# Two distance layers of a fused four-layer kernel: weights written at another place, squares and box sums in parts, three taps of the second half ahead of the products of sums

## The reference

```python
def _conv_dt(x, centers):                       # centers: [O, C*9]
    patches = lax.conv_general_dilated_patches(x, filter_shape=(3, 3), ..., padding=((1, 1), (1, 1)))
    p = patches.transpose(0, 2, 3, 1).reshape(-1, C * 9)
    p2 = jnp.sum(p * p, axis=-1, keepdims=True)
    c2 = jnp.sum(centers * centers, axis=-1)
    d2 = p2 - 2.0 * (p @ centers.T) + c2
    d = jnp.sqrt(jnp.maximum(d2, D2_EPS))
...
out = jax.nn.relu(_bn(_conv_dt(x, centers1), gamma1, beta1))
out = _bn(_conv_dt(out, centers2), gamma2, beta2)
return jax.nn.relu(out + x)
```

## Time and profile before

| | |
|---|---|
| median of 3 runs | 768.92 us (766.22 to 769.92) |
| profiled execution | 763.28 us |
| its span in the trace | 761.1 us |
| mean granted TensorE clock | 0.915 of full speed |
| last addition of the deformable layer ends | 670.07 us |
| first distance layer, first tap to last statistics | 672.36 to 704.03 us |
| second distance layer, first tap to last statistics | 714.63 to 749.09 us |

### The profile page before, as it was taken

The page is one execution under the profiler, slowest core; times in us unless marked ns, Lnnn a source line. Parts: engine busy times, 40 slices in busy tenths (PEclk is TensorE's granted clock), DMA queues, the critical chain, the costliest instruction groups (busy, mean ns, idle before and its releaser), DMA issues.

```text
span 761.1 us, 29083 instructions
## 1 busy us (share of the span) xinstructions
PE 591.4 (78%) x13260; PEld 412.2 (54%) x13260; DVE 627.5 (82%) x811; ACT 486.0 (64%) x680; POOL 144.3 (19%) x246
## 2 busy tenths in 40 slices
PE   2628999699886799888886779678888888467591
PEld 1215788484653576666554555456666655345260
DVE  5997999993457999999998336899999999795356
ACT  2715565223227999999993413899999999332514
POOL 1013000000241333334200034133344320000000
PEclk9959999899987899999999798899999999879596
DMA  5013000000678788887720068889788770000002
GB/s 202 0 29 84 4 3 4 18 4 19 170 225 346 244 287 273 267 275 259 247 93 3 3 183 265 315 242 340 239 262 266 270 258 14 2 2 3 1 3 111
DMA packets 30197, 111.10 MB, mean 146 GB/s; under 512 B 11140, under 2 KB 15940, under 8 KB 25976
## 3 DMA queue, kind: packets, MB, share of 16 engines
q0 software_dynamic: 14912, 87.85, 34.1%
q1 hardware_dynamic: 15160, 21.36, 9.3%
HBM read 92.19 MB, written 19.65 MB: 147 GB/s over the span
## 4 chain that ended last, share of the span: by engine, by line
DVE 29%; PE 26%; ACT 25%; issue 8%; DMA 8%; SPq 3%; POOL 0%; DVEq 0%; ACTq 0%; POOLq 0%
PE psum L1438 7%; ACT arena L1201 6%; DVE arena L709 5%; ACT arena L1211 5%; ACT arena L1200 5%; PE psum L1587 4%; DMA offsets<-arena 4%; PE psum L1385 4%; PE psum L1472 4%; DMA arena<-offsets_by_batch 3%; ACT arena L1184 3%; ACT arena L1191 3%; PE psum L1496 2%; SPq L508 2%; DVE arena L837 2%
## 5 line engine op out<-in xcount | busy, mean ns | idle before, releaser
L1472 PE MATMUL psum<-arena 64*64 64x297 f32 (+4 forms) x4512 | 231.8, 350 | 55.5 <-DVE arena L837 45.7
L1472 PEld LDWEIGHTS psum<-arena 64*64 64x64 f32 x4512 | 170.8, 138 | 124.7 <-DVE arena L837 63.3
L1664 POOL DMA_DIRECT2D arena<-offsets_by_batch x128 | 79.4, 633 | 210.9 <-DVE arena L837 150.2
L1438 PE MATMUL psum<-arena 32*32 32x512 f32 x2304 | 88.4, 657 | 20.4 <-issue 14.5
L1385 PE MATMUL psum<-arena 32*32 32x512 f32 x2592 | 96.3, 614 | 8.1 <-DVE arena L689 8.1
L835 DVE SCALAR_TENSOR_TENSOR arena<-arena 128x792 f32<-128x792 f32 (+3 forms) x96 | 92.6, 964 | 12.0 <-ACT arena L1201 11.0
L1211 ACT ACTIVATE arena<-psum 128x792 f32<-128x792 f32 (+1 forms) x96 | 89.4, 931 | 14.5 <-PE psum L1477 9.0
L1201 ACT ACTIVATE arena<-arena 128x792 f32<-128x792 f32 (+3 forms) x96 | 93.4, 973 | 0.0
L1200 ACT ACTIVATE arena<-arena 128x792 f32<-128x792 f32 (+3 forms) x96 | 93.1, 970 | 0.0
L837 DVE SCALAR_TENSOR_TENSOR arena<-arena 128x792 f32<-128x792 f32 (+3 forms) x96 | 92.4, 962 | 0.0
L836 DVE SCALAR_TENSOR_TENSOR arena<-arena 128x792 f32<-128x792 f32 (+3 forms) x96 | 92.3, 962 | 0.0
(11 more groups left out here) (161 smaller groups left out, 726.0 us busy)
## 6 DMA issues: line engine op xcount, KB each, us to landing
arena<-offsets_by_batch POOLq DMA_DIRECT2D x112, 576.0 KB, 8.0
arena<-offsets_by_batch POOLq DMA_DIRECT2D x16, 624.0 KB, 7.6
offsets<-arena SPq DMA_DIRECT2D x32, 256.0 KB, 10.5
offsets_by_batch<-offsets SPq DMA_DIRECT2D x184, 24.0 KB
arena<-columns POOLq DMA_DIRECT2D x24, 160.0 KB, 9.6
columns<-arena POOLq DMA_DIRECT2D x8, 320.0 KB
arena<-in_x SPq DMA_DIRECT2D x4, 512.0 KB, 5.3
out<-arena SPq DMA_DIRECT2D x8, 256.0 KB, 2.2
```

Source lines behind the costliest of these rows:

```text
L1438: ins = t_.matmul(ps_q(2 * axis + h, conv_bank(m) + i), cols(W_CONV[L] + (axis * K + t) * Q, Q, Q * i, Q), ap(XA + (BLK * m + 8 * h + t // ...
L1472: ins = t_.matmul(ps_t(s, bank + r, first * K * w, many * K * w), window, ap(g_at(unit, d0) + first * TW + s * w, [[GS + TW, many], [SLOTS ...
```

## The change

- `distance_weights(0)` moves from behind the deformable layers to the start of the second of them, ahead of `bound_offsets`. Its weights lie where the first deformable layer's weights were. `distance_weights(1)` moves between the two halves of the first distance layer.
- First distance layer: squares in two parts (35 and 33 rows) and box sums in two parts (34 and 32 rows).
- Input of the second layer: pairs 0 and 1 on ScalarE as before, pairs 2 and 3 on VectorE (`second_input`: a multiply-add and a maximum).
- Second distance layer: the squares of each pair's 16 inner rows by themselves, pairs 0 and 1 ahead of ScalarE's border copies and pairs 2 and 3 behind them, then those of the border rows; box sums in the same five parts.
- TensorE takes the taps in the order 3 to 8, then 0 to 2. In the second layer it waits for the border copies only ahead of the seventh tap. Three taps of the second half stand ahead of the first half's products of sums.

```diff
+        W_DT = [place(K * P, MATS), place(K * P, SAMP)]
+        JUNK = [MATS + K * P, SAMP + K * P]
+        SPLIT = PW // 2 + 1
...
             def layer2(L):
+                if L == 1:
+                    distance_weights(0)
                 bound_offsets(L, 0)
...
+            def box(L, rows, pitch, src, dst):
+                sq = lambda dx: ap(src + dx, [[pitch, rows], [1, W]])
+                hs = ap(dst, [[W, rows], [1, W]])
+                link(v.tensor_tensor(hs, sq(0), sq(1), ALU.add))
+                return v.tensor_tensor(hs, hs, sq(2), ALU.add)
+            def boxes_of_images():
+                for part, (first, end) in enumerate(((0, SPLIT), (SPLIT, PW))):
+                    dve.wait_ge(s_sq, part + 1)
+                    box(0, end - first, XW, SQ3 + (first + 1) * XW + 1, HS3 + first * W).then_inc(s_box, 1)
+            def boxes_of_pairs():
+                for i in range(4):
+                    dve.wait_ge(s_sq, 2 + i + 1)
+                    box(1, REGION, PW, SQ3 + i * PAIRN + PW, HS3 + (i * RP + 1) * W).then_inc(s_box, 1)
+                dve.wait_ge(s_sq, 7)
+                sq = lambda dx: ap(SQ3 + dx, [[PAIRN, 4], [(RP - 1) * PW, 2], [1, W]])
+                hs = ap(HS3, [[RP * W, 4], [(RP - 1) * W, 2], [1, W]])
                 link(v.tensor_tensor(hs, sq(0), sq(1), ALU.add))
                 v.tensor_tensor(hs, hs, sq(2), ALU.add).then_inc(s_box, 1)
...
+                    if L == 0 and c == 0:
+                        distance_weights(1)
...
+            def second_input():
+                dve.wait_ge(s_cz, 1)
+                dve.wait_ge(s_coef, 4)
+                part = lambda i: ap(XP3 + i * PAIRN + PW + 1, [[PW, REGION], [1, W]])
+                for i in (2, 3):
+                    ins = v.tensor_scalar(part(i), ap(D3 + 2 * i * CH, [[W, REGION], [1, W]]), cols(NC_, 1),
+                                          cols(NC_ + 1, 1), ALU.mult, ALU.add)
+                link(ins)
+                for i in (2, 3):
+                    v.tensor_scalar(part(i), part(i), 0.0, None, ALU.max).then_inc(s_x3v, 1)
...
-            dve.wait_ge(s_xa, 3 * NCH)
-            distance_weights(0)
-            distance_weights(1)
+            boxes_of_images()
             distance(0)
+            second_input()
             copy_lower_borders()
+            boxes_of_pairs()
             distance(1)
...
-                    act.wait_ge(s_xa, 3 * NCH)
-                    a.activation(cols(SQ3, XN), cols(XA, XN), ACT.Square).then_inc(s_sq, 1)
+                    for first, end in ((0, SPLIT + 1), (SPLIT + 1, XW)):
+                        act.wait_ge(s_xa, 2 * NCH + (5 if first == 0 else NCH))
+                        a.activation(cols(SQ3 + first * XW, (end - first) * XW), cols(XA + first * XW, (end - first) * XW),
+                                     ACT.Square).then_inc(s_sq, 1)
                 else:
+                    inner = lambda buf, i: cols(buf + i * PAIRN + PW, REGION * PW)
+                    act.wait_ge(s_x3, 2)
+                    for i in range(2):
+                        a.activation(inner(SQ3, i), inner(XP3, i), ACT.Square).then_inc(s_sq, 1)
                     act.wait_ge(s_hp, 2)
...
                     ins.then_inc(s_ha, 1)
+                    act.wait_ge(s_x3v, 2)
+                    for i in (2, 3):
+                        a.activation(inner(SQ3, i), inner(XP3, i), ACT.Square).then_inc(s_sq, 1)
                     act.wait_ge(s_ha, 1)
                     act.wait_ge(s_hv, 1)
-                    a.activation(cols(SQ3, 4 * PAIRN), cols(XP3, 4 * PAIRN), ACT.Square).then_inc(s_sq, 1)
+                    border = lambda buf: ap(buf, [[PAIRN, 4], [(RP - 1) * PW, 2], [1, PW]])
+                    a.activation(border(SQ3), border(XP3), ACT.Square).then_inc(s_sq, 1)
...
-                    for i in range(4):
+                    for i in range(2):
...
-                pe.wait_ge(s_x3, 4)
+                pe.wait_ge(s_x3, 2)
+                pe.wait_ge(s_x3v, 2)
...
-                for c in range(2):
-                    for k in range(K):
+                def taps(c, first, end):
+                    for step in range(first, end):
+                        k = (step + 3) % K
+                        if L == 1 and step == 6 and c == 0:
+                            pe.wait_ge(s_ha, 1)
+                            pe.wait_ge(s_hv, 1)
...
-                        pe.wait_ge(s_box, L + 1)
+                        pe.wait_ge(s_box, 2 if L == 0 else 7)
...
+                taps(0, 0, K)
+                if L == 1:
+                    pe.wait_ge(s_d2, NCH)
+                taps(1, 0, 3)
+                norms(0)
+                taps(1, 3, K)
+                norms(1)
...
                     move_borders()
-                    pe.wait_ge(s_ha, 1)
-                    pe.wait_ge(s_hv, 1)
```

More of the change, by code:

```diff
@@ L306, in build @@
         s_hp, s_ha, s_hv = sem("border_rows_moved"), sem("borders_by_scalar"), sem("borders_by_vector")
-        s_x3, s_fin, s_res = sem("second_input_ready"), sem("final_sums_ready"), sem("results_ready")
+        s_x3, s_x3v = sem("second_input_by_scalar"), sem("second_input_by_vector")
+        s_fin, s_res = sem("final_sums_ready"), sem("results_ready")
         block = ctx.enter_context(nc.Block())
@@ L389, in build @@
         assert OUT3 + N <= XA
-        W_DT = [place(K * P, SAMP), place(K * P, SAMP + K * P)]
-        JUNK = SAMP + 2 * K * P
+        W_DT = [place(K * P, MATS), place(K * P, SAMP)]
+        JUNK = [MATS + K * P, SAMP + K * P]
+        assert (K + 2) * P <= (2 + NT) * P + NGRP * Q
+        SPLIT = PW // 2 + 1
         def xa_rows(ch):
@@ L998, in distance_weights @@
                                 ALU.mult).then_inc(s_dw3, 1)
-                link(v.tensor_tensor_reduce(cols(JUNK, K * C), cols(WR + WREP[f"cn{L}"][0], K * C),
+                link(v.tensor_tensor_reduce(cols(JUNK[L], K * C), cols(WR + WREP[f"cn{L}"][0], K * C),
                                             cols(WR + WREP[f"cn{L}"][0], K * C), 1.0, 0.0, ALU.mult, ALU.add,
@@ L1040, in _, with distance @@
                 layer2(L)
[L1043 to L1051, removed]
+            def box(L, rows, pitch, src, dst):
[14 more added lines that the diff above has]
+                hs = ap(HS3, [[RP * W, 4], [(RP - 1) * W, 2], [1, W]])
                 link(v.tensor_tensor(hs, sq(0), sq(1), ALU.add))
                 v.tensor_tensor(hs, hs, sq(2), ALU.add).then_inc(s_box, 1)
+            def distance(L):
                 for c in range(2):
@@ L1587, in distances, with norms @@
                                 t_.matmul(ps_q(j, 4 * c + i), cols(W_DT[L] + k * P + Q * i, Q, Q * i, Q), at,
-                                          start=(k == 0), stop=False)
+                                          start=(step == 0), stop=False)
+                def norms(c):
                     if c == 0:
-                        pe.wait_ge(s_box, L + 1)
+                        pe.wait_ge(s_box, 2 if L == 0 else 7)
                     for ky in range(3):
```

## The result

| | before | after |
|---|---|---|
| median of the runs | 767.57 us (4 runs) | 753.79 us (749.62 to 754.98, 4 runs) |
| ratio of the runs | | 0.9845, 95% interval 0.9807 to 0.9883 |
| profiled execution, its span | 763.28, 761.1 us | 754.98, 753.1 us |
| mean granted clock | 0.915 | 0.924 |

The direction is right, and every step is there, but the sum is too small, and the 768.92 us that it was taken from lay high.

The account below looks back on a forecast made before the run. No single engine was taken to bound the kernel; its last 92 us were a chain of waits hardly overlapping. Gains of 2.2 + 3.1 + 1.7 = 7.0 us, from a 768.92 us median, gave 761.9 us, range 758 to 766.5.

Parts of the forecast that it names:

- Part 1 and 2: First distance layer: weights written earlier start the taps 2.2 us sooner; split squares and box sums keep that gain.
- Nothing waits: First distance layer of the kernel before: nine taps end as the box sums end, about 683.6 us, without any wait.
- 0.38 us: Both distance layers: cost of each further microsecond of TensorE at 1.2 GHz, from taps of 1.70 against 1.06 us.
- Part 3: Second distance layer's input split between ScalarE and VectorE: ready after 3.0 us instead of 4.65, 1.6 us earlier.
- T+3.1: Second distance layer: start of the border products, 3.1 us after T, the moment the coefficients are there.
- Rival B: VectorE's new instructions run at the full-length rate: second input 5.0 instead of 3.0 us, total 763.9 us; chance 0.08.
- Part 4: Second layer's taps start before the border copies: 3.1 us earlier, 1.6 from the split input and 1.5 from the copies.
- Border products: T+3.1 to T+4.3: Second layer: border products take 1.19 us after the input is ready, and TensorE's taps begin at T+4.3.
- Part 5: Second layer's squares and box sums in five parts: TensorE's 1.7 us standstill before the products of sums is gone.
- rival A: TensorE's clock rises when it did though taps start earlier: 2.0 us less gain, 763.9 us; chance 0.20.
- Rivals C and D: C: a misjudged wait undoes parts 3 to 5, 766.7 us, 0.09; D: 1.2 GHz through both first halves, 773.5 us, 0.03.

Follow-up runs that it names:

- e9: Changed kernel with the first distance layer's weights written behind the last addition of the deformable layers again; 755.78 us, ratio 0.9859 to the kernel before.
- e3: Kernel before with only the placement of both distance layers' weights changed; 765.83 us, ratio 1.0012 to the kernel before.
- e1: Kernel before run again without any edit, beside itself; 765.87 us against 764.18, ratio 1.0014.
- e16: Kernel before, unedited, one profiled execution for a fifth trace; 93.6 us behind the last addition of the deformable layers.
- e10: Kernel before with four filler products ahead of TensorE's wait for the second layer's box sums; ratio 0.9994 to the kernel before.
- e13: Kernel before with filler products on TensorE between the distance layers, around the group sum and behind the border products; 764.62 us, ratio 0.9991.
- e7: Changed kernel with the second layer's squares in one instruction and its box sums whole again; 756.26 us, ratio 0.9875 to the kernel before.
- e6: Changed kernel with the second layer's wait for border copies ahead of the first tap, not the seventh; 757.39 us, ratio 0.9888 to the kernel before.
- e12: Changed kernel run a third time without any edit; 753.36 us, ratio 0.9856 to the kernel before.
- e5: Changed kernel with the second layer's input written by ScalarE alone in four pieces; 756.61 us, ratio 0.9890 to the kernel before.
- e4: Changed kernel with no taps of the second half ahead of the first half's products of sums; 758.17 us, ratio 0.9889 to the kernel before.
- e2: Changed kernel run again without any edit; 752.06 us, ratio 0.9831 to the kernel before.
- e15: Kernel before, unedited, one profiled execution for a fourth trace; 93.0 us behind the last addition of the deformable layers.
- e8: Changed kernel with filler products keeping TensorE busy ahead of both distance layers; 751.52 us, ratio 0.9804 to the kernel before.
- e11: Kernel before run a third time without any edit; 764.95 us, ratio 0.9989 to the kernel before.

## Why the prediction was wrong

The mechanisms were right; two terms of the sum were too small. One charged taps with a wait that only the border copies have. The other was read from a single trace and took the profile's idle time for the whole loss.

**Part 1 and 2, 2.2 us: right in the mean.** Stage A shows 2.3 (means), e9 1.9, and e3 shows that without the parts none of it arrives. Two readings behind it were off. "Nothing waits" in the kernel before hid a wait: its first products of sums began at 683.66, 0.05 us behind the box sums, while the last product of the nine taps, 0.59 us long, ended at 683.92 and so had begun 0.3 us before these. Its stage A stays at 28.9 us for low stretches of 3.0 to 4.2 us (before, e1, e16, e10, e13) and is longer only at 5.4 and 5.8 (29.2, 29.3). And a microsecond of the low clock costs more than 0.38 us where TensorE waits for nothing: stage A of the changed kernel's versions goes from 25.9 at 3.0 us (e7) to 27.5 at 6.2 (e6), 0.5 us for each. So the gain of the stage depends on the clock: in after's trace, with 5.8 us low, it is 1.6 us against before's, in e12's, with 3.4, it is 2.8.

**Part 3, 1.6 us: right.** The multiply-adds took 0.77 us and the maxima 0.65, for 0.75 and 0.69 forecast; T+3.1 for the border products is what the trace shows (709.28 - 706.17). e5 gives 1.7. Rival B is out.

**Part 4, "3.1 us earlier": mis-sized, 4.3.** The step that failed is "Border products: T+3.1 to T+4.3", with the taps behind it. The 1.19 us from the earlier trace rows run from the first border product to the copies, which read what these products write. The taps read none of it for six steps: they entered 0.05 us behind the first border product. e6 sizes the edit at 2.6 us where 1.5 was charged; with the 1.7 of e5 that is the 4.3 of stage B.

**Part 5, "the standstill of 1.7 us": mis-sized, about 4.** This is the larger of the two failed steps. The standstill was taken from one trace, which had the longest low stretch of the five (6.0 us), so the slowest taps and the shortest standstill. The five show 1.71, 1.80, 2.65, 2.67 and 3.09 us, 2.4 on average. In three of them the clock fell behind it, and the first operation of VectorE came 4.8, 4.8 and 5.8 us behind the first product of sums in place of 3.2: 1.2 us on average over the five. That makes 3.5 of the 4.1 us of stage C. The other 0.6 is what the idle time leaves out: the profile counts it from the end of the taps' last product, 727.07 in before's trace, and this product, 0.59 us long, began at 726.48, so from start to start it is 2.3 us and not 1.71. Without a wait this tail costs nothing: in after's trace the first products of sums (723.78) come ahead of a tap's product that starts at 723.92. It is the oversight of part 4 once more, with the same figure in every trace, but no run was made for it alone. In e4, which has no fall of the clock, the standstill and this tail make 1.9 of the 2.4 us; the other 0.5 I didn't separate. The prediction asked what a longer low stretch costs the changed kernel (rival A), and not what a shorter one costs the kernel before.

**Rival A** itself shows in single traces (5.8 us in after's first layer) but not as a rule: the changed kernel's six low stretches average 4.5 us, the ten of the kernel before 4.6.

**The measure.** The sum was set against one profiled execution; its A to D is 1.3 us under the mean of five. Against 92.4 the traces give 10.7 us, or 0.986, which lies in the intervals of after (0.9807 to 0.9883), e2 and e12. The medians' 13.8 us is 3 more than that, with four runs on each side. Over all runs the means are 765.3 us (111 executions of the kernel before) and 754.05 (16 of the changed one), 11.2 apart. I take 10.7 to 11.2 as what the change is worth, and the rest as scatter. So of the 8.1 us between the forecast of 761.9 and the 753.79 measured, some 4 are the two terms, and 3.6 are the 768.92 us of three executions that the forecast started from. From the 765.3 us of all executions the forecast would have been 758.3 us, still 4.5 above what was measured.

**Rivals C and D** are out in all three traces of the changed kernel: no wait was left over (no idle time before step 6 or before the products of sums; in after's trace the box sums were 1.0 us ahead of these), and no low stretch came near 18 us.

What stays open: where the scatter ahead of the last addition comes from. In e2's trace the second deformable layer took 249.6 us and in before's 244.7; between 460 and 500 us VectorE was busy 27.5 us in the one and 33.4 in the other. The trace of e15, the latest of the kernel before, has the same 27.5 us, and in these two the DMA engines moved 271 and 285 GB/s in that stretch, in the other six traces of the two kernels 291 to 295. So the lost time seems to go with slower transfers. No experiment was made on it.

## What to carry to other kernels

A standstill of TensorE is worth more than the profile's idle time: by the 0.6 us that the last product was still under way here, and by more where the granted clock falls behind it. Whether it does must be read from several traces, for the moment at which the clock rises shifts the standstill itself. Ahead of a wait whose end is set by another engine, work that doesn't need the result (three taps of the next half) takes away both the wait and the fall; speeding up TensorE in front of such a wait gained nothing (e13) until the other engine is off the path, and then it did (e8). Count a start by what the next instruction waits for: the time from a product to its reader is not the time to the next product.

## What the runs showed of the hardware

Where the clock was low at a layer's first tap, it stayed so for 3.0 to 6.2 us in 32 stretches of 17 traces, with no relation to which kernel ran. Where the second layer's products of sums stood behind a wait of TensorE, the clock fell behind 1.87, 2.65, 2.67, 3.05, 3.09 and 4.41 us of idle time (e7, e11, e15, e3, e16, e13) and didn't behind 1.34, 1.71 and 1.80 us (e4, before, e1). The length of the idle time alone doesn't decide it: in e8, where TensorE had been kept busy before, the granted clock stayed at 1.00 behind 2.46 us of idle time ahead of the first tap and 2.08 us ahead of the three fillers. What else enters wasn't tested.

A product of 32 x 32 by 512 columns is under way for 0.59 us in the profile, which gives modelled ends for TensorE, and the next group starts behind the last product's start and not its end where nothing is waited for.
